# Gating, scaling and inverse roots of a delta-rule layer's output: GpSimd's work given to VectorE and ScalarE in the last step

## What is computed

```python
xn = _layernorm(x)
q, k, v = silu(causal conv of xn @ qk_w.T, xn @ vg_w.T)       # q, k normalised by head
def step(S, inp):                                             # for each row t
    S = S * exp(g_t)
    delta = (v_t - k_t S) * b_t
    S = S + k_t delta^T
    return S, q_t S                                           # o_t
eps = jnp.finfo(o.dtype).eps
o = o * jax.lax.rsqrt(jnp.mean(o * o, axis=-1, keepdims=True) + eps)   # mean over the 32 of a head
o = o * jax.nn.silu(g_out)
attention = o.reshape(Bm, Tm, VAL_DIM) @ o_w.T
return x + attention + feed_forward(xn)
```

## Time and profile before

| | us |
|---|---|
| median of three runs | 3283.02 |
| lowest, highest | 3282.77, 3287.08 |
| profiled execution, its own time | 3294.0 |
| its span, first to last instruction | 3292.1 |
| busy in it: TensorE, VectorE, GpSimd, ScalarE | 3120.8, 2497.7, 1921.5, 1673.7 |
| busy from 3228 on (64.1 us): TensorE, VectorE, GpSimd, ScalarE | 35.17, 11.93, 11.41, 17.09 |

### The profile page before, as it was taken

The page is one execution under the profiler, slowest core; times in us unless marked ns, Lnnn a source line. Parts: engine busy times, 40 slices in busy tenths (PEclk is TensorE's granted clock), DMA queues, the critical chain, the costliest instruction groups (busy, mean ns, idle before and its releaser), DMA issues.

```text
span 3292.1 us, 117601 instructions
## 1 busy us (share of the span) xinstructions
PE 3120.8 (95%) x45504; PEld 2217.6 (67%) x45504; DVE 2497.7 (76%) x5504; ACT 1673.7 (51%) x3338; POOL 1921.5 (58%) x2961
## 2 busy tenths in 40 slices
PE   5999999999999999999999999999999999999986
PEld 4666676666666766676666766666667666767664
DVE  7777777777777777778777777777777777777762
ACT  4544555544555545555445555445555445554452
POOL 4566555666555666556665556665556665556643
PEclk8999999999999999999999999999999999999996
DMA  3000000000000000000000000000000000000000
GB/s 119 8 21 15 12 18 21 21 21 15 9 21 21 21 21 6 18 21 21 21 21 5 18 21 21 21 15 9 21 21 21 21 9 15 21 21 21 15 4 19
DMA packets 34301, 64.95 MB, mean 20 GB/s; under 512 B 5360, under 2 KB 7152, under 8 KB 33776
## 3 DMA queue, kind: packets, MB, share of 16 engines
q1 hardware_dynamic: 29808, 52.13, 4.8%
q10 hardware_dynamic: 4096, 6.42, 0.6%
HBM read 41.76 MB, written 16.78 MB: 18 GB/s over the span
## 4 chain that ended last, share of the span: by engine, by line
PE 76%; DVE 12%; issue 7%; ACT 3%; POOL 1%; ACTq 1%; DVEq 0%; POOLq 0%
PE PS L1193 15%; PE PS L1146 14%; PE PS L1180 8%; PE PS L1181 7%; PE PS L1404 7%; PE PS L1265 7%; DVE arena L897 5%; PE PS L1330 3%; PE PS L1248 3%; DVE arena L984 2%; PE PS L1283 2%; PE PS L1382 2%; DVE arena L381 2%; PE PS L1205 1%; PE PS L1301 1%
## 5 line engine op out<-in xcount | busy, mean ns | idle before, releaser
L897 DVE SCALAR_TENSOR_TENSOR arena<-PS,sc,arena 128x256 f32<-128x256 f32 x2112 | 1002.6, 481 | 405.1 <-ACT arena L603 218.3
L1180 PE MATMUL PS<-xh,wgu 128*128 128x256 f32 x2816 | 880.8, 345 | 32.7 <-DVE arena L897 20.9
L603 ACT ACTIVATE arena<-PS,sc 128x256 f32<-128x256 f32 x704 | 329.8, 473 | 753.0 <-PE PS L1181 753.0
L1181 PE MATMUL PS<-xl,wgu 128*128 128x256 f32 x2816 | 702.4, 282 | 0.0
L1193 PE MATMUL PS<-wdn,inner 128*128 128x512 f32 x1408 | 656.3, 592 | 0.0
L1180 PEld LDWEIGHTS PS<-xh,wgu 128*128 128x128 f32 x2816 | 532.1, 189 | 179.4 <-issue 71.8
L500 POOL TENSOR_TENSOR work<-arena 128x31 f32<-128x31 f32 (+15 forms) x992 | 521.8, 526 | 133.7 <-DVE arena L984 58.4
L1181 PEld LDWEIGHTS PS<-xl,wgu 128*128 128x128 f32 x2816 | 533.3, 189 | 83.6 <-issue 83.6
L504 POOL TENSOR_TENSOR arena<-arena,work 128x31 f32<-128x31 f32 (+15 forms) x992 | 543.0, 547 | 77.9 <-POOL work L500 0.2
L1146 PE MATMUL PS<-xnT,wqkv 128*128 128x256 f32 x2048 | 491.7, 391 | 9.3 <-ACT inner L583 9.3
L1146 PEld LDWEIGHTS PS<-xnT,wqkv 128*128 128x128 f32 x2048 | 382.9, 193 | 76.4 <-issue 13.6
(11 more groups left out here) (153 smaller groups left out, 4683.1 us busy)
## 6 DMA issues: line engine op xcount, KB each, us to landing
xt<-in_x SPq DMA_DIRECT2D x64, 256.0 KB, 3.2
obuf<-in_x SPq DMA_DIRECT2D x64, 256.0 KB, 2.7
out<-obuf SPq DMA_DIRECT2D x64, 256.0 KB, 2.0
wqkv<-in_wqkv ACTq DMA_DIRECT2D x1, 2048.0 KB, 14.2
arena<-in_gup ACTq DMA_DIRECT2D x2, 704.0 KB, 6.9
arena<-in_dns SPq DMA_DIRECT2D x1, 1408.0 KB, 12.2
wg<-in_wg ACTq DMA_DIRECT2D x1, 1024.0 KB, 19.9
wo<-in_wo ACTq DMA_DIRECT2D x1, 1024.0 KB, 17.2
```

The source lines that it names most:

```text
L603: eng.activation(fa[:, u % 4, :], PS[:, bank(u, 0), 0:NB * P], ACT.Copy, scale=sc[:, u % 2, KB * m:KB * m + 1]).then_inc(fa_scaled.sem, 1)
L897: eng.scalar_tensor_tensor(out=fa[:, u % 4, :], in0=PS[:, bank(u, k // 2), k % 2 * NB * P:][:, 0:NB * P], scalar=sc[:, u % 2, KB * m + k:K ...
L1180: eng.matmul(o, w, xh[:, k, :], start=True, stop=False)
L1181: ins = eng.matmul(o, w, xl[:, k, :], start=False, stop=True)
```

## The change

In the last step (n is None) GpSimd does nothing more. VectorE, right behind its sums of squares, makes the means plus eps in `ro`, gates both blocks and scales both (`last_output`, new). ScalarE makes the inverse roots in between, as exp(-0.5 * ln(ro)): it loads the tables of the logarithm behind its second square, waits for the means, takes the logarithm, loads the tables of the exponential, takes it, and only then copies the turned blocks. Three signals are new. And the six loads of tables of `act_step` are made only in a step with a new tile, so that the last step has none of them. Every other step is as it was.

```diff
--- before.py
+++ after.py
@@ -295,6 +295,9 @@
         decay_out = signal("decay_out", 2)
         gu_out = signal("gu_out", 2 * NU)
         pu_out = signal("pu_out", 1)
+        last_means = signal("last_means", 0)
+        last_logs = signal("last_logs", 0)
+        last_roots = signal("last_roots", 0)
         qk_turned = signal("qk_turned", 2)
         o_turned = signal("o_turned", 2)
         wo_out = signal("wo_out", 2)
@@ -543,7 +546,7 @@
                 clear_solution(eng, n)
                 if more:
                     layer_norm_scale(eng, n.next())
-            if t:
+            if t and n:
                 gated_and_scaled(eng, t)
             if n:
                 solve(eng, n)
@@ -699,7 +702,8 @@
                                ACT.Exp).then_inc(decay_done.sem, 1)
 
 
-            eng.preload_act_table_set(EXP)
+            if n:
+                eng.preload_act_table_set(EXP)
             if n:
                 eng.wait_ge(*ab_parts_out.at(n, 1))
                 eng.activation(abT, PS[:, 6, 0:NB * P], ACT.Copy).then_inc(ab_copied.sem, 1)
@@ -708,13 +712,15 @@
             if n:
                 eng.wait_ge(*zabs_done.at(n, 1))
                 eng.activation(ee[:, :, :], zz[:, :, :], ACT.Exp).then_inc(ee_done.sem, 1)
-            eng.preload_act_table_set(LOG)
+            if n:
+                eng.preload_act_table_set(LOG)
             project(2)
             if n:
                 eng.wait_ge(*ee_done.at(n, 1))
                 eng.activation(lnz[:, :, :], ee[:, :, 0:H], ACT.Ln, bias=1.0).then_inc(lnz_done.sem, 1)
             project(3)
-            eng.preload_act_table_set(SILU)
+            if n:
+                eng.preload_act_table_set(SILU)
             qk_silu(0)
             qk_silu(1)
             project(4)
@@ -769,6 +778,12 @@
                     eng.wait_ge(*o_copied.at(t, b + 1))
                     eng.activation(osq[:, b, :], sq[:, b, :], ACT.Square).then_inc(osq_done.sem, 1)
             if not n:
+                eng.preload_act_table_set(LOG)
+                eng.wait_ge(last_means.sem, 1)
+                eng.activation(ro[:, :, :], ro[:, :, :], ACT.Ln).then_inc(last_logs.sem, 1)
+                eng.preload_act_table_set(EXP)
+                eng.wait_ge(last_logs.sem, 1)
+                eng.activation(ro[:, :, :], ro[:, :, :], ACT.Exp, scale=-0.5).then_inc(last_roots.sem, 1)
                 o_columns()
                 return
             eng.wait_ge(*taps_done.at(n, NQKV))
@@ -932,6 +947,19 @@
                 eng.wait_ge(*wo_out.at(t, b + 1))
                 eng.tensor_tensor(obuf[:, b, :], obuf[:, b, :], PS[:, 6 + b, :], ALU.add).then_inc(attn_added.sem, 1)
 
+            def last_output():
+                eng.wait_ge(*so_done.at(t, NB))
+                eng.tensor_scalar(ro[:, :, :], so[:, :, :], 1.0 / DV, float(np.finfo(np.float32).eps), ALU.mult,
+                                  ALU.add).then_inc(last_means.sem, 1)
+                eng.wait_ge(*gs_done.at(t, 1))
+                for b in range(NB):
+                    eng.tensor_tensor(sq[:, b, :], sq[:, b, :], gs[:, b, :], ALU.mult).then_inc(o_gated.sem, 1)
+                eng.wait_ge(last_roots.sem, 1)
+                for b in range(NB):
+                    eng.wait_ge(*o_gated.at(t, b + 1))
+                    oh = sq[:, b, :].rearrange("p (h v) -> p h v", v=DV)
+                    eng.tensor_tensor(oh, oh, bc(ro[:, b, :], DV), ALU.mult).then_inc(o_scaled.sem, 1)
+
             def keep_rows(b):
 
                 if not n:
@@ -1064,6 +1092,8 @@
                     eng.wait_ge(*osq_done.at(t, b + 1))
                     eng.tensor_reduce(so[:, b, :], osq[:, b, :].rearrange("p (h v) -> p h v", v=DV), AX.X,
                                       ALU.add).then_inc(so_done.sem, 1)
+                if not n:
+                    last_output()
             gram_products(0)
             gram_products(1)
             unit(3)
```

## The result

The changed kernel takes 3281.44 us (median of 21 runs, 3274.77 to 3295.77). The kernel before was measured further beside it: over 21 runs, its first three among them, it takes 3288.87 us (3278.33 to 3293.03), not 3283.02 us. The ratio of the two is 0.9982, with a 95% interval from 0.9973 to 0.9990: 5.9 us faster, and something between 3.3 and 8.9 us (the medians lie 7.4 us apart, the means 5.6 us). The forecast of a difference, 5.2 us, lies well inside this interval. The range of the forecast time, 3276.0 to 3281.9 us, holds the measured 3281.4 at its upper edge, but by luck, as the part on the prediction shows. And the prediction, which did write "though a real gain", took the outcome "within 0.2%" for one that a measurement can't tell from no change. The measured gain is within 0.2%, and the measurement does tell it from no change.

What follows compares the result with a forecast made beforehand. The prediction took the last step for a latency chain gated by GpSimd; with table loads and VectorE's scaling in its place the turn came 5.2 us sooner, other terms 0, so 3283.02 - 5.2 = 3277.8 us, range 3276.0 to 3281.9.

Steps and rivals of the forecast that it cites:

- The chain, and what takes its place: Last step, squares to turn: two 1.28 us loads, logarithm, exponential and scaling replace GpSimd's work; turn at 3271.8, not 3277.04.
- The later of two inputs: Before the logarithm: the table load ends about 0.2 us after VectorE's means and sets the logarithm's start.
- The hidden gates: VectorE's two gates, 0.69 us each, end 0.7 us before the roots; the worst price would cost some 0.4 us.
- The removed loads: Six table loads in the last step lie in ScalarE's waits for TensorE; removal taken as 0, at most 0.1 us.
- What is next: From the turn on: block 1 is never late, the work is the same, so the end shifts whole by 5.2 us.
- The drain at a table load: Rival, chance 0.04: each table switch on ScalarE's path costs more than its load, giving 3280.4 us.
- The clock: Rival, chance 0.18: TensorE's clock rises sooner after the turn, saving up to 1.45 us more, giving 3276.3 us.
- The slower loop: Rival, chance 0.03: each of thirty loop passes loses time; 0.17 us a pass cancels the gain, 0.39 gives about 3290 us.
- the last step, from the sum to the verdict: Whole kernel: 5.2 us, 0.16%, held against a 0.2% (6.6 us) measuring bound; verdict "within 0.2%", chance 0.77.
- The level: Whole kernel's absolute time: the 5.2 us taken off the earlier runs' median, 3283.02 us, giving 3277.8 us.

Runs made afterwards that it cites:

- the work moved: Changed kernel with the six table loads put back in the last step; ratio to the kernel before 0.9986 (0.9973 to 0.9999), 12 runs.
- the loads left out: Kernel before with only the last step's six table loads left out; ratio to the kernel before 1.0003 (0.9993 to 1.0014), 12 runs.
- the repeat: Changed kernel measured a second time without edit, 3303.51 us against 3308.23 us for the kernel before; ratio 0.9981 (0.9971 to 0.9992).
- through the last step, again: Changed kernel with one table set, block-by-block scaling and added matmuls in TensorE's idle places all through the last step; ratio to kernel before 0.9971.

## Why the prediction was right, and where it was wrong

**The chain, and what takes its place: right.** The loads from 3263.32, the logarithm, the second load, the exponential, the scaling stand in the predicted order. Counted from the end of the squares the predicted times were: first load's end 1.30 us, exponential's end 3.06, turn 3.9 us; measured 1.30, 3.08 and 3.86 us (3263.30, 3264.60, 3266.38, 3267.16).

**The later of two inputs: right.** The means were predicted 0.2 us ahead of the load; they were 0.22 us ahead, and taking the load away brought 0.20 us.

**The hidden gates: right.** VectorE waited 0.84 us for the roots, against 0.7 us predicted, and gated two blocks in 1.28 us.

**The removed loads: right.** 0 us taken, up to 0.1 allowed, 0.04 measured; a kernel with that part alone has the ratio 1.0003.

**What is next: right.** Block 1 isn't late, and the turn to the end is 11.75 us against 11.77.

**The drain at a table load: it isn't there.** The logarithm starts 0.01 us after its load (3263.32 + 1.28 = 3264.60, 3264.61), the exponential 0.01 us after the second, and each load starts 0.02 us behind the instruction before it. The Trainium skill's page on ScalarE (ScalarE: Activation LUTs, What ACT_TABLE_LOAD costs) has about 1380 ns more for a switch, and on this path both switches would have shown it.

**The clock: the size right, its part in the difference none.** Ten profiles in which it rose after the turn, from 3.3 to 6.1 us behind it, give 10.4 to 11.8 us from the turn to the end, half a us for each us of delay. The prediction's rival was that the changed kernel's rise would be sooner; in the first pair of profiles the two were alike to 0.03 us, so that rival has no part in the 5.3 us. Where the clock rose in the other executions isn't recorded, so whether it has one in the 5.9 us stays open.

**The slower loop: no sign of it.** Thirty passes took 2995.3 us before and 2995.9 us in the changed kernel, 0.02 us a pass, where the rival needed 0.17; and the intervals of the ratios of the changed kernel (twice), of the work moved and of the loads left out hold what their tails show.

**What failed is the last step, from the sum to the verdict.** The sum was 5.2 us, and the tail's measured difference is 5.3. The step that failed is the term "about 0.2%, 6.6 us, is what a measurement of this kernel can tell from no change". The prediction held its 0.16% against this bound, gave "within 0.2%" a chance of 0.77 and treated the outcome as one that a measurement couldn't tell from no change. It can, with enough runs: 21 of each gave an interval of plus and minus 0.09%, 2.8 us, and the repeat plus and minus 0.10%; both exclude 1. The bound was taken for a property of the kernel when it is one of the number of runs. Three runs of each, with the spread of the 21 (standard deviations of 4.0 and 5.2 us), would give about plus and minus 7 us, 0.2%, by an estimate from these figures. The sign, which each step of the working supported, should have been the forecast, with "too small to see" as a matter of how many runs there are.

**The level was the second fault, and luck covered it.** The absolute time was hung on the median of three runs, 3283.02 us. The same kernel's 21 runs have a median of 3288.87 us, and the later measurements, on four chips, 3308.23 us (35 runs), 3311.77 us (29 runs), 3310.49 us (15 runs) and 3310.8 us (one run). From 3288.87 the same sum gives 3283.7 us, 1.8 us above the forecast range. The prediction saw the one run at 3287.08 us, had no cause for it in the profile, and widened its upper end for it; that, and a median of the changed kernel 2.2 us below 3283.7, kept 3281.4 inside the range. Neither was foreseen, so that hit is luck. A cause for such differences can be seen in a profile. These are the starts of GpSimd's power in three passes of the changed kernel's loop, and windows from one to the next (from:to, length, TensorE busy, its clock, DMA):

```profile
2269.37 5.43 POOL L530 TENSOR_TENSOR ro<-ro,mhalf 128x32 f32<-128x32 f32 x1 [0.28 <-POOL ro L527]
...
2369.02 5.44 POOL L530 TENSOR_TENSOR ro<-ro,mhalf 128x32 f32<-128x32 f32 x1 [0.28 <-POOL ro L527]
...
2471.08 5.43 POOL L530 TENSOR_TENSOR ro<-ro,mhalf 128x32 f32<-128x32 f32 x1 [0.28 <-POOL ro L527]
...
2269.40:2369.00 99.60, 96.32 (x1424) 1.00 0.05 18
2369.00:2471.10 102.10, 98.95 (x1423) 0.97 0.05 17
```

The pass takes 99.6 us where the clock stays at 2.4 GHz, and 102.1 us where the clock fell within it (share 0.97 over the pass). Where and how often it falls differs between executions of one kernel: the mean clock of the changed kernel's span is 0.985 in its first profile and 0.981 in the second, and the spans are 3282.3 and 3302.7 us. Over the 21 executions of the changed kernel the time goes with the mean clock: 0.988 has 3276.6 to 3280.8 us, 0.987 has 3274.8 to 3280.0, 0.985 has 3278.7 to 3286.1, 0.984 has 3284.6 to 3291.3, 0.982 has 3295.8 us. The groups overlap, so the clock isn't shown to be all of the spread, and no experiment tested it. Nor is it shown why the later measurements lie 20 us higher; the record doesn't say on which chip the first one was made. It is this spread, of some 20 us, that three runs can't resolve and a tail of 5 us is measured against.

## What to carry to other kernels

Where a kernel ends in a chain with a single instruction at work at a time, sum the chain instruction by instruction from rows of the same size: here every link came out within 0.1 us. Replace a slow function on one engine (5.43 us for 128x32 powers on GpSimd) only after asking which of the new inputs comes last, and look at what idle engines could prepare: a table set that has both functions, loaded in an earlier wait, took a further 0.9 us from the path, and scaling block 0 before gating block 1 another 0.4, of which half was lost behind the turn. And before comparing a difference of a few us with "what can be measured", find the spread between executions of one kernel and its cause, since the number of runs moves that bound.

## What the runs showed of the hardware that was not expected

- VectorE's multiply and add on 128x32 elements took 0.18 us with GpSimd idle and 1.19 us, until 0.04 us behind GpSimd's end, while GpSimd multiplied blocks of 128x512; its sums over 128x512 beside the same work took 1.28 us as ever.
- GpSimd's power over 128x32 elements took 5.43 to 5.44 us all 32 times in the kernel before, and 5.80 us once, as GpSimd's first instruction after 40 us without work and beside VectorE's gates.
- TensorE's clock was at 2.4 GHz and fell to 1.2 GHz at 3231.92 before, 0.25 us behind the 3.85 us in which TensorE waits at the start of the last step, and at 3225.42 in the changed kernel, within that wait. Where added matmuls fill the wait to 0.46 us (through the last step, again) it fell only at 3252.22. The small matmuls of the recurrence (32x32 tiles, with gaps of up to 2.3 us) didn't bring it back for good: in the profile before and the first one of the changed kernel it stayed at 1.2 GHz until 6.1 us behind the turn's start, and in four others it rose and fell again, as in the changed kernel's second profile from 3279.29 to 3282.70, with only 32x32 matmuls at work. With added 128x128 matmuls it rose 4.5 us after they began. Small matmuls gain from the higher level too: a chunk of the recurrence took 4.0 to 4.1 us instead of 4.5.
- Waits put down to "issue" in TensorE's P·U, a run of some 250 matmuls of 32x32, sum to 1.86 us in the changed kernel and 2.95 in the one with the work moved alone, though both have the same program of TensorE. The wait of ScalarE for P·U, with a table load in it where there is one, was between 7.8 and 8.9 us over all kernels.
